# First product of the graph convolution for two streams at once, in passes of 512 columns

## The reference

```python
h = relu(einsum('ts,bsh->bth', adj, x @ Wg0 + bg0))
h = relu(einsum('ts,bsh->bth', adj, h @ Wg1 + bg1))
```

## Time and profile before

| | us |
|---|---|
| median of 3 executions | 2177.47 (2176.42 to 2178.97) |
| the profiled execution | 2180.21 |
| its span, first to last instruction | 2177.6 |
| convolution turns 1 to 7 on PE, first product to the last mixing | 651.86 to 764.93 |
| one turn in the steady state | 16.17 |
| PE busy in the span | 2106.6 (97%) |

### The profile page before, as it was taken

One profiled execution on the slowest core, in us unless ns is written; L12 is line 12 of the kernel. 1 busy time (PEld: TensorE's weight loads), 2 busy tenths in 40 slices (PEclk: granted clock), 3 DMA queues, 4 the chain that ended last, 5 costly groups with the idle time before them and its releaser, 6 DMA issues. The chain is left out here.

```text
span 2177.6 us, 43993 instructions
## 1 busy us (share of the span) xinstructions
PE 2106.6 (97%) x17941; PEld 1844.0 (85%) x17941; DVE 1364.5 (63%) x2736; ACT 1155.9 (53%) x2184; POOL 459.2 (21%) x1132
## 2 busy tenths in 40 slices
PE   6999999999989999999999999999999999889998
PEld 4999899989979978888888999988888799777886
DVE  5788888888876744533334434354443589876775
ACT  1554465445544467644344434353443477657987
POOL 3455555555530000000000000000000122003343
PEclk9999999999999999999999999999999999999999
DMA  4001111111122110000000000000000143001333
GB/s 126 20 26 50 55 36 40 50 55 36 45 91 90 39 51 20 1 20 1 1 1 20 20 1 1 1 1 20 1 1 1 54 128 112 1 20 50 81 86 78
DMA packets 77080, 83.08 MB, mean 38 GB/s; under 512 B 7136, under 2 KB 74592, under 8 KB 76000
## 3 DMA queue, kind: packets, MB, share of 16 engines
q1 hardware_dynamic: 76896, 80.53, 12.5%
HBM read 55.34 MB, written 25.17 MB: 37 GB/s over the span
## 5 line engine op out<-in xcount | busy, mean ns | idle before, releaser
L332 PE MATMUL ps<-R 128*128 128x256 f32 (+3 forms) x8136 | 1492.3, 343 | 16.2 <-DVE R L903 7.9
L332 PEld LDWEIGHTS ps<-R 128*128 128x128 f32 x8136 | 1309.9, 190 | 174.3 <-DVE R L903 8.7
L1481 ACT ACTIVATE late_half<-ps,lstm_bias 128x512 f32<-128x512 f32 (+2 forms) x460 | 283.0, 669 | 374.4 <-PE ps L332 374.4
L374 POOL TENSOR_TENSOR ln_veps<-ln_mv,eps_tile 128x2 f32<-128x2 f32 x128 | 25.0, 195 | 1195.8 <-DVE ln_mv L357 1195.8
L301 POOL TENSOR_TENSOR H<-H 128x128 f32<-128x128 f32 x384 | 188.9, 525 | 68.3 <-DVE H L944 68.3
L1551 DVE TENSOR_TENSOR late_half<-late_half 128x1024 f32<-128x1024 f32 (+2 forms) x32 | 37.6, 1176 | 183.5 <-ACT late_half L1481 183.5
L1475 ACT ACTIVATE late_half<-late_half 128x1024 f32<-128x1024 f32 (+2 forms) x66 | 68.1, 1031 | 124.5 <-DVE late_half L1556 78.4
L1044 PE MATMUL ps<-H 128*128 128x256 f32 x512 | 124.8, 387 | 0.8 <-ACT H L731 0.8
L1553 DVE TENSOR_TENSOR late_half<-late_half 128x1024 f32<-128x1024 f32 (+2 forms) x32 | 37.6, 1175 | 131.1 <-ACT late_half L1481 131.1
L1068 PE MATMUL ps<-H 128*128 128x256 f32 x512 | 117.2, 379 | 0.0
L1068 PEld LDWEIGHTS ps<-H 128*128 128x128 f32 x512 | 95.6, 190 | 12.7
(11 more groups left out here) (217 smaller groups left out, 2544.0 us busy)
## 6 DMA issues: line engine op xcount, KB each, us to landing
H<-in_x SPq DMA_DIRECT2D x64, 256.0 KB, 3.0
residual<-H SPq DMA_DIRECT2D x32, 256.0 KB, 2.2
H<-residual SPq DMA_DIRECT2D x32, 256.0 KB, 3.0
arena<-residual SPq DMA_DIRECT2D x32, 256.0 KB, 2.8
residual<-arena SPq DMA_DIRECT2D x32, 256.0 KB, 2.1
H_state<-residual SPq DMA_DIRECT2D x32, 256.0 KB, 2.9
out<-H_state SPq DMA_DIRECT2D x64, 128.0 KB, 2.4
arena<-in_wih SPq DMA_DIRECT2D x4, 1024.0 KB, 5.4
```

The lines of the kernel that those rows point to most:

```text
L332: mm = pe.matmul(out, lhsT(a), rhs(b), start=start and n == 0, stop=stop and n == len(PASSES) - 1)
L1481: ins = act.activation(into[q][:, m, 0:x.cols], gate_ps(q, m, x.cols), ACT.Tanh if q == TANH_G else ACT.Sigmoid, bias=lstm_bias[:, x.p - 1 ...
```

## The change

From turn 1 on, FIRST is done for two streams at once. The pairs are streams 0 and 1, and streams 2 and 3. The operands of the two streams lie side by side in one piece of SBUF (`fm_words`), and a matmul takes 256 columns of one stream and 256 of the other, 512 in all. Its output fills one whole bank: output block m=0 goes to the second bank of the even stream, m=1 to the second bank of the odd one. PE issues 12 matmuls of 512 columns for a pair, in the place where the even stream's own matmuls stood; nothing is issued in the place of the odd stream, where only its wait is left. DVE's `add_mixed_bias` reads for a stream its half of both banks, and waits for both. Turn 0 is unchanged, as are the arithmetic and the weights.

```diff
-    fm = [w0r(2, KD, GROUP) for _ in S]
+    PAIRS = STREAMS // 2
+    fm_words = [w0r(2 * 2 * KD * GROUP) for _ in range(PAIRS)]
+    fm_pair = [v.rearrange("p (s q k n) -> p s q k n", s=2, q=2, k=KD) for v in fm_words]
+    fm = [fm_pair[s // 2][:, s % 2] for s in S]
...
+    def paired(s):
+
+        pair = ps[:, 2 * BANKS * (s // 2):2 * BANKS * (s // 2 + 1), :]
+        return pair.rearrange("p (m b) w -> p m b w", b=BANKS)[:, :, BANKS - 1, :]
+
+    def paired_out(s, m):
+
+        return paired(s)[:, m, :].rearrange("p (s n) -> p s n", s=2)
+
+    def paired_part(s):
+
+        return paired(s)[:, :, GROUP * (s % 2):GROUP * (s % 2 + 1)]
...
             def add_mixed_bias(s, turn):
                 dve.wait_ge(g0_done[s], turn + (g0_base + 1))
+                products = feature_major(s, 1)
+                if not first(turn):
+                    products = paired_part(s)
+                    dve.wait_ge(g0_done[s ^ 1], turn + (g0_base + 1))
                 for k in range(KD):
                     nb = GROUP // NODES
-                    by_block = (tg_f[s][:, k, :], feature_major(s, 1)[:, k, :])
+                    by_block = (tg_f[s][:, k, :], products[:, k, :])
...
                     pe.wait_ge(zg_ready[s], turn + (zg_base + 1))
-                    for m in range(KD):
-                        for k in range(KD):
-                            mm = exact_mm(pe, feature_major(s, 1)[:, m, :],
-                                          lambda q: wg_r[:, q, 0, k, m * P:(m + 1) * P],
-                                          lambda q: zg[s][:, q, k, :], k == 0, k == KD - 1)
-                    mm.then_inc(g0_done[s], 1)
+                    if first(turn):
+                        for m in range(KD):
+                            for k in range(KD):
+                                mm = exact_mm(pe, feature_major(s, 1)[:, m, :],
+                                              lambda q: wg_r[:, q, 0, k, m * P:(m + 1) * P],
+                                              lambda q: zg[s][:, q, k, :], k == 0, k == KD - 1)
+                        mm.then_inc(g0_done[s], 1)
+                    elif s % 2 == 0:
+                        for m in range(KD):
+                            for k in range(KD):
+                                mm = exact_mm(pe, paired_out(s, m), lambda q: wg_r[:, q, 0, k, m * P:(m + 1) * P],
+                                              lambda q: zg_pair[s // 2][:, :, q, k, :], k == 0, k == KD - 1)
+                            mm.then_inc(g0_done[s + m], 1)
```

More of the change, by code:

```diff
@@ L532, in build_program @@
     zg = fm
+    zg_pair = fm_pair
     wg_r = w0r(2, 2, KD, D)
```

## The result

The changed kernel took 2183.97 us (median of 7 executions, 2182.59 to 2186.17) and the kernel before 2177.57 us (7 executions): the ratio is 1.0028 with a 95% interval of 1.0018 to 1.0037, so it is slower by 0.28%; the medians are 6.4 us apart. (The ratios in this document come from all executions of a job, and differ from the quotient of two medians by up to 0.0005.) The forecast of 2179.7 is 4.3 us short, and the time lies 1.2 us above the range. The direction and, for the steady turns, the kind of loss are as forecast, the size is not. In a second job, on a chip where the kernel before took 2179.87 us (31 executions), the changed one took 2184.47 us, +4.6 (ratio 1.0023, 1.0014 to 1.0033).

The account below looks back on a forecast made before the run. PE, busy 97% of the span, was taken as the bound. Passes -0.41, start +0.60 and wait +0.21 gave +0.40 us in six turns, with -0.20 in turn 2: 2177.47 + 2.2 = 2179.7 us, range 2176.4 to 2182.8.

Parts of the forecast that it names:

- The start: Turn's first matmul waits for the splits of streams 3 and 2, not 3 alone: +0.60 us a turn.
- The wait ahead of SECOND: SECOND of stream 2 waits for its split, queued on DVE behind bias 1: +0.21 us a turn.
- Part 1: FIRST's passes: 24 matmuls of 512 columns replace 48 of 256, 17 ns saved each, -0.41 us a turn.
- The two-piece operand: Larger matmul's operand in two pieces, taken as costing 0; rival that it costs the 17 ns: 2182.5 us, chance 0.03.
- Turn 2: Turn after PE's 1.27 us stop: the later start costs nothing there, so -0.20 us; no change of the stop taken.
- code comes elsewhere: Rival: PE's stop in the loop's first passage goes or comes twice, 1.3 us either way, 2178.4 or 2181.0; chance 0.06.
- Part 3: Between FIRST and SECOND: a new wait for stream 2's split, +0.21 us a turn, bounds 0 and about 0.5.
- the clock doesn't fall in the gaps: Against the rival that 1.08 us idle at turn starts lowers the clock, 1.31 us at five turns: 2186; chance 0.03.
- the turn of 16.57 us: Sign expected in the profile after: a turn of 16.57 us in place of 16.17.
- the full clock in turn 2: Sign expected in the profile after: granted clock at 1.00 throughout turns 2 to 7.
- The case for slower: Whole kernel slower by more than 0.2% (4.35 us): chance 0.18, of which 0.10 for the order on DVE.
- a wait of 0.57 us ahead of SECOND: Rival that DVE's order bites harder: 0.57 in place of 0.21 reaches the 0.2% line; 2182 to 2184, chance 0.10.

Follow-up runs that it names:

- with one semaphore: Changed kernel without the odd stream's own wait on PE, so one matmul waits for one semaphore: 2183.44 us, ratio 1.0020.
- The kernels with the code put back: Changed kernel plus 48 semaphore increments on PE, ahead of the loop (2184.28 us, ratio 1.0020) or at the program's very start (2186.18 us, ratio 1.0038).

## Why the prediction was wrong

**The three terms of a turn.** The mechanism was right and each size a little off. The start was put at 0.60 and measured 0.68 us: the spacing of the splits was right (0.59 with one semaphore), the second semaphore's 0.09 was missing. The wait ahead of SECOND was put at 0.21 and measured 0.27; place and cause were right, since PE's weight loads wait for that split, and moving the one split on DVE took the wait away. The passes were put at -0.41 and measured -0.30. Here the step was wrong (Part 1): I divided the distance from the run to the mixing by 96 and got 121.9 ns, but this distance holds the entry and the end of the run too. DVE's row biases, each released by one stream's SECOND, give the pace from the inside, here in turn 6 of the kernel before:

```profile
744.01 0.69 DVE L922 TENSOR_TENSOR H<-ps,arena 128x512 f32<-128x512 f32 x1
745.45 0.69 DVE L922 TENSOR_TENSOR H<-ps,arena 128x512 f32<-128x512 f32 x1 [0.75 <-PE ps L332]
...
746.88 0.69 DVE L922 TENSOR_TENSOR H<-ps,arena 128x512 f32<-128x512 f32 x1 [0.75 <-PE ps L332]
```

Twenty-four matmuls take 746.88 - 744.01 = 2.87 us, 119.6 ns each, so two small ones are 239 and a large one saves 12 to 13 ns and not 17. The two-piece operand costs nothing: the rate is the LSTM's. Together 0.68 + 0.27 - 0.30 = 0.65 us a turn, where I had 0.40. All three errors had the same sign. For the six turns that gives 3.9 instead of 2.4 us, 1.5 of the 4.3 us that were missed.

**Turn 2.** This is the larger part. I had -0.20 for it and put the stop's change at nothing ("I take none"). The run from its first matmul to the mixing would have been 11.67 us, nearly nothing gained or lost, but it came to 13.28, with a stop 0.9 us longer ahead of it. That is 1.6 + 0.9 and, with the stop's surroundings (664.23 to 670.96 is 6.73 us, and was 5.51), up to 2.8 us. The kernels with the code put back, where this stretch is 5.65 and 5.68 us and the run 11.7, agree: 1.1 + 1.6 = 2.7. In the prediction this stood as the rival "code comes elsewhere", with 1.3 us either way and a chance of 0.06. Its mechanism was seen and its price was not: I took the clock out of the account because it had stayed up after a stop of 1.27, and then let the stop grow without asking what the clock does after 2.2.

**The sum.** 6 x 0.65 + 2.5 to 2.8 = 6.4 to 6.7 us. The first job's medians are 6.4 apart and the second's 4.6; the intervals of the two ratios are +3.9 to +8.1 us and +3.1 to +7.2. So the account fits both jobs, and that it meets the first so closely is partly luck. On the part of the profile that the change touches, +6.43 divides into 5 x 0.68 for the starts of turns 3 to 7, -0.15 for their runs, +0.35 for turn 1's run (which differs by more between two executions of the kernel before: 13.02 and 13.82), +1.58 for turn 2's and +1.22 for the stretch with the stop. Turn 1's own later start lies ahead of this part and isn't in it. The part as a whole took 110.97 and 112.11 us in two executions of the kernel before, and 117.1 to 117.5 in three of the changed one.

The range was too narrow for the same reasons. Its upper end, 2182.8, gave the stop 1.3 us and Part 3 six turns, where the wait comes in seven; its lower end, 2176.4, comes out at 2176.5 from the terms that it names.

**What was right.** The passes are worth a tenth of a percent at most; the loss of a steady turn is one of waiting; the clock doesn't fall in the gaps of 1.16 us at the turns' starts (granted 1.00 from 689.40 to the end of turn 7); the change does what it says. Of the signs that I had named, the turn of 16.57 us and the full clock in turn 2 failed. The case for slower had been tied mainly to a wait of 0.57 us ahead of SECOND, which didn't come (it is 0.27), and so had 0.18 in all: too little, because errors of 0.1 us in each of three terms, times six turns, already bring the +2.2 to +4.0, close to the line of 4.35, and the stop's term was open.

## What to carry to other kernels

When a wider instruction joins the work of two streams, count first what each half had to wait for: the first pass now waits for the later half's operand, and everything that consumed the first half early moves to the end of both. Here that was 0.95 us a turn against 0.30 gained. Join only where both operands are long ready and look which instruction in the consumers' fixed order now stands behind the later product; and take the pace of a short run from its inside, not from its ends.

## What the runs showed of the hardware

A matmul of 256 columns of this kernel runs at 119.6 ns and one of 512 at 226.7 ns. The 256 further columns cost 107.1 ns, so 12 to 13 ns of a matmul don't depend on its width. With a wait for a second semaphore ahead of the matmul PE stood idle for 0.09 us longer (1.16 for 1.07), although the first of the two had been passed one split, 0.6 us, earlier. A loop shorter by twenty-four matmuls and their weight loads had its stop in the first passage at another place. There it took 1.92 to 2.17 us in five of six executions, where it takes 1.18 to 1.56 in the eight with the code elsewhere. In the turn after stops of 1.92 us and more the granted clock fell to half, after those of 1.56 us and less it did not.
